# Loops over blocks in the first graph layer's sums, written out on four engines

## The chip, the cores and the metric

The kernel runs on one core of one Trainium2 chip. Time is device microseconds from the start to the end of one execution, and the lower the better. Five engines work side by side, each with its own list of instructions: PE (matrix products), DVE (vector), ACT (scalar and activation), POOL (here it issues the gathering DMAs) and SP (here it issues all other DMAs). They meet at semaphores.

## The reference, cut to what matters

Four graph layers run one after the other on 6250 nodes of 128 features and 200,000 edges. The change is in the first, a gated update from weighted means over neighbours in both directions:

```python
neigh1 = _weighted_mean_agg(feat, w, src, dst, n)   # sum of w * feat[src] by dst, over sum of w
neigh2 = _weighted_mean_agg(feat, w, dst, src, n)   # sum of w * feat[dst] by src, over sum of w
hn = jnp.concatenate([neigh1 @ W1.T, neigh2 @ W2.T], axis=1)
gi = hn @ w_ih.T + b_ih
gh = feat @ w_hh.T + b_hh
...
return nn_ + z * (feat - nn_)
```

The code's own name for the stage is stage_gru_sums: it makes the two sums (msum and wsum) for every node, in both directions.

## The kernel before, in words

The edges lie sorted by their target. They are cut into cells of up to 128 edges, where each cell has two target nodes, and 64 cells make a batch: NBATCH is 74, and the stage goes through the 74 batches in order. For a batch of number n, there are 16 steps q (HALVES), and this is what happens in them.

- Cells. DVE builds one-hot matrices for 8 cells at a time (L733, L738, L743: koh, loh, kw). PE multiplies them (make_cells, L813 to L821), four cells in each step q, into ps_cell. ACT copies the result to X (L798), a ring of 8 slots. SP stores X to the chip's memory, turned (store, L621 to L625): 16 stores of 196 KB for a batch, and each counts up one of four semaphores `stored`, a quarter of the batch each.
- Backward. SP loads the stored batch again, in another order, as AT (load_turned, L627 to L632): 8 loads of 392 KB, numbers 0 to 5 in the steps q = 9 to 14 of the same batch, numbers 6 and 7 in the steps q = 1 and 2 of the next. Load 6 waits for the last quarter, which means for the landing of store 15. With all eight landed, PE multiplies AT by the gathered target rows (backward, L823 to L833): 17 groups for a batch, from step q = 6 of the next batch on. DVE adds each group to x (L700).
- Forward. POOL gathers the source rows (L672), ACT makes one-hots and weights rows (L774, L777, L783), PE sums them (sum_run, L835 to L844, six for each batch), DVE adds to fwd (L717) at a bucket's number that it loads from memory into a register (run_bucket, L551 to L555).

Each engine has a function body(i, bb), which issues the whole work of batch n = 2 i + bb on this engine; the function asks known(n) to leave out batches that there aren't. over_bodies (L606) calls it. For i = 0 and 1 the calls are made while the program is written, so that n is a whole number and every column and semaphore value is a constant. From i = 2 to 36 over_batches (L528) makes a loop of the engine (`eng.Fori`) round two calls (bb = 0 and 1). There i is a register: each semaphore value that depends on n is worked out by the engine's sequencer ahead of the wait (ALU_OP, FUSED_REGOPS), as are the columns in key_tab, lo_tab, w_tab and run_save. At its end the loop has one branch back. For i = 37, which only finishes what is left of batch 73, the calls are written out again. POOL's list has no loop: it is written out for all 74 batches.

The order in which the work of an engine stands is written by hand, and there is no planner. SP's queue is one list, in which a load that waits holds up the stores behind it.

Of the kernel before, what the change touches and what calls it, by code (L numbers as in the profile page):

```python
# [45 lines left out]
NBATCH = -(-(ET + GROUPS - 1) // HALF)  # L46
# [72 lines left out]
def build(nc, a, out_x):  # L119
# [10 lines left out]
    def sem(name):  # L130
        stage_sems.append(nc.alloc_semaphore(name))
        return stage_sems[-1]
# [26 lines left out]
    with es:  # L159
# [368 lines left out]
        def over_batches(eng, body, tail=None, peeled=1):  # L528

            for i in range(peeled):  # L530
                for bb in range(2):
                    body(i, bb)
            with eng.Fori(peeled, NBATCH // 2) as i:
                for bb in range(2):
                    body(i, bb)
            if tail is not None:
                tail()
# [19 lines left out]
        def stage_gru_sums(fwd, key_tab, lo_tab, w_tab, dst_tab):  # L557
# [5 lines left out]
            with ExitStack() as ctx:  # L563
# [26 lines left out]
                runs_in = [sem(f"g_runs_in{b}") for b in range(2)]  # L590
                rows_in = [sem(f"g_rows_in{b}") for b in range(GR)]

                def known(n):

                    return not isinstance(n, int) or 0 <= n < NBATCH
# [8 lines left out]
                    return range(TG * k, min(TG * (k + 1), BUCKETS))  # L604

                def over_bodies(eng, body):  # L606
                    over_batches(eng, body, peeled=2)
                    for bb in range(2):
                        body(NBATCH // 2, bb)

                with nc.Block() as block:
                    @block.sync
                    def _(sp):
                        def load_runs(n, bb):

                            if not (isinstance(n, int) and n < 2):
                                sp.wait_ge(weighted, RPB * (n - 1))
                                sp.nop(nofuse=True)
                            sp.dma_start(runs[:, bb, :, :], run_save[:, :, bass.ds(n * RD, RD)]).then_inc(runs_in[bb], 16)

                        def store(n, bb, q):  # L621

                            sp.wait_ge(evacd, HALVES * n + q + 3)
                            sp.dma_start(turn_save[bb, CQ * q:CQ * (q + 1), :, :].rearrange("c k l -> k c l"),
                                         X[0:KEYS, q % XR, :].rearrange("k (c l) -> k c l", c=CQ)).then_inc(stored[q // QT_HALVES], 16)  # L625

                        def load_turned(m, b, y):  # L627

                            sp.wait_ge(stored[y // 2], 16 * QT_HALVES * (m + 1))
                            sp.nop(nofuse=True)  # L630
                            sp.dma_start(AT[y:P:EIGHTHS, b, :],
                                         turn_save[b, HALF // EIGHTHS * y:HALF // EIGHTHS * (y + 1), :, :].rearrange("c (j h) l -> (c j) (h l)", j=GRP)  # L632
                                         ).then_inc(turned[b], 16)

                        def body(i, bb):
                            n = 2 * i + bb
                            if known(n):
                                if isinstance(n, int) and n == 0:
                                    load_runs(n, bb)
                                if known(n - 2):  # L640
                                    sp.wait_ge(turned[bb], 16 * EIGHTHS * i)
                                    sp.nop(nofuse=True)
                            for q in range(HALVES):
                                if known(n):
                                    store(n, bb, q)
                                if q in (1, 2) and known(n - 1):
                                    load_turned(n - 1, 1 - bb, EIGHTHS - 3 + q)
                                if known(n) and 9 <= q < 15:
                                    if q == 9 and known(n - 2):
                                        sp.wait_ge(rev_made, TGS * (n - 1))  # L650
                                        sp.nop(nofuse=True)
                                    load_turned(n, bb, q - 9)
                                if q == 5 and known(n) and known(n + 1):
                                    load_runs(n + 1, 1 - bb)

                        over_bodies(sp, body)
                        sp.wait_ge(runs_in[0], 16 * (NBATCH // 2 + 1))

                    @block.gpsimd
                    def _(g):  # L660
# [24 lines left out]
                    def _(v):  # L685
# [62 lines left out]
                        def body(i, bb):  # L748
                            n = 2 * i + bb
                            for cc in range(CB):  # L750
# [7 lines left out]
                                add_run(n_then, s + 1)  # L758

                        over_bodies(v, body)  # L760

                    @block.scalar
                    def _(s):
# [23 lines left out]
                        def body(i, bb):  # L787
                            n = 2 * i + bb
                            for q in range(HALVES):
# [9 lines left out]
                                if known(n):  # L799
                                    if q in OH_AT:  # L800
                                        make_run_oh(i, n, bb, OH_AT[q])
                                    if q in SCALE_AT:
                                        weigh_run(n, bb, SCALE_AT[q])

                        over_bodies(s, body)

                    @block.tensor
# [1822 lines left out]
```

## Time and profile before

| | us |
|---|---|
| median of 3 runs | 9322.11 |
| lowest and highest run | 9304.29, 9326.89 |
| profiled execution, its own time | 9326.77 |
| its span (first to last instruction) | 9325.0 |
| PE, DVE, ACT, POOL busy in it | 8295.5, 5838.0, 5420.3, 4943.9 |

The profile's page has a picture of 40 slices, 233 us each, with busy shares in tenths. The stage of the change takes slices 1 to 12: it starts at about 125 us with the first loads, and its last backward group starts at 2805 us. PE's digit is 9 from slice 2 on in it, and DVE's and DMA's 8. The row of a stretch shows the same in numbers: busy us of each engine with the number of its instructions, then the granted TensorE clock (PEclk, 1 is full speed), the mean share for which the 16 DMA engines were busy, and GB/s. PE shows matrix products, PEld the weight loads beside them; an engine's name with a q is its sequencer. In a list in order of time, the bracket says how long the engine had been idle before, and who ended it.

### The profile page before, as it was taken

The numbers are of one execution on the slowest core, as the hardware profiler recorded it, in microseconds if no ns is written. First come the engines' busy times: TensorE is split into PE (matmuls) and PEld (weight loads), VectorE is DVE, ScalarE is ACT, GpSimd is POOL, SyncE is SP. The second block draws the span as 40 slices with busy tenths as digits, with TensorE's granted clock in tenths as the row PEclk, the third lists the DMA queues.
The fourth block names the chain that finished last, engine by engine and source line by source line (L and its number), as shares of the span: only waits on it lengthen the run. The fifth ranks groups of instructions, "written<-read, shape, count | busy, mean of one in ns | idle before, by whom it ended". The sixth has DMA issues, their size and how long they took to land. (4 is left out here: it accounts for less than half of the span.)

```text
span 9325.0 us, 221484 instructions
## 1 busy us (share of the span) xinstructions
PE 8295.5 (89%) x54969; PEld 6586.8 (71%) x54970; DVE 5838.0 (63%) x12428; ACT 5420.3 (58%) x14197; POOL 4943.9 (53%) x5229
## 2 busy tenths in 40 slices
PE   5999999989897999989988888888885999999998
PEld 4888888888884777766656666666663666666666
DVE  6888888888885777751145555555554555555555
ACT  5777777777774444430026767676754555555555
POOL 5666666666660000000007777777760777777775
PEclk8999999999998999999989999999997999999999
DMA  6888888888881222235544444444430222222222
GB/s 193 224 227 226 227 224 227 226 226 227 225 226 43 111 110 117 110 125 192 190 143 116 118 118 118 118 118 118 118 112 28 74 73 73 73 73 73 73 73 69
DMA packets 963534, 1294.60 MB, mean 139 GB/s; under 512 B 187018, under 2 KB 821186, under 8 KB 934210
## 3 DMA queue, kind: packets, MB, share of 16 engines
q1 hardware_dynamic: 769858, 837.45, 30.7%
q0 software_dynamic: 193536, 455.41, 17.7%
q8 instruction: 73, 1.20, 0.1%
q14 instruction: 67, 0.55, 0.0%
HBM read 906.61 MB, written 385.62 MB: 139 GB/s over the span
## 5 line engine op out<-in xcount | busy, mean ns | idle before, releaser
L1823 POOL DMA_INDIRECT x<-table,p_gidx x1632 | 1546.5, 948 | 2377.7 <-ACT p_gidx L1860 1957.9
L672 POOL DMA_INDIRECT g_G<-table,g_runs x1776 | 1686.5, 950 | 769.9 <-issue 479.5
L2275 POOL DMA_INDIRECT c_G<-table,c_gidx x1632 | 1548.4, 949 | 505.2 <-issue 497.1
L820 PE MATMUL g_ps_cell<-g_loh,g_kw 128*98 128x128 f32 x9472 | 1254.1, 277 | 29.2 <-DVE g_kw L743 29.2
L831 PE MATMUL g_ps_rev<-g_hrow,g_AT 128*128 128x129 f32 x7252 | 1054.6, 284 | 192.3 <-DMA g_AT<-turn_save 155.1
L820 PEld LDWEIGHTS g_ps_cell<-g_loh,g_kw 128*98 128x98 f32 x9472 | 1127.5, 168 | 29.7 <-DVE g_kw L743 29.4
L1913 PE MATMUL p_ps_sum<-x 128*96 128x256 f32 x3264 | 898.4, 398 | 231.5 <-DVE hid L1849 221.3
L798 ACT COPY g_X<-g_ps_cell 98x512 f32<-98x512 f32 x1184 | 681.4, 576 | 720.8 <-PE g_ps_cell L820 697.9
L831 PEld LDWEIGHTS g_ps_rev<-g_hrow,g_AT 128*128 128x128 f32 x7252 | 930.2, 197 | 239.9 <-issue 184.0
L1913 PEld LDWEIGHTS p_ps_sum<-x 128*96 128x96 f32 x3264 | 468.7, 163 | 646.0 <-ACT x L1878 260.3
L1849 DVE TENSOR_TENSOR hid<-hid,p_ps_sum 96x256 f32 x1632 | 678.0, 415 | 375.2 <-DVE hid L1849 372.1
L1840 DVE TENSOR_TENSOR x<-x,p_ps_pre 128x512 f32<-128x512 f32 x816 | 524.1, 684 | 498.0 <-DMA x<-table,p_gidx 493.4
L1385 ACT CAST a_A<-a_ps_cell 128x392 bf16<-128x392 f32 x1184 | 511.0, 492 | 542.7 <-PE a_ps_cell L1419 542.7
L1903 PE MATMUL p_ps_pre<-own,p_lhs 128*128 x3264 | 785.6, 384 | 9.9 <-issue 1.7
L2339 ACT ACTIVATE c_pos<-c_ps_lin,c_b 128x512 f32<-128x512 f32 x408 | 280.5, 688 | 872.5 <-PE c_ps_lin L2362 872.5
L700 DVE TENSOR_TENSOR x<-x,g_ps_rev 128x387 f32<-128x387 f32 (+1 forms) x1258 | 639.8, 535 | 228.5 <-PE g_ps_rev L831 228.3
L2314 DVE TENSOR_TENSOR acc<-acc,c_ps_sum 96x128 f32 x1632 | 462.5, 283 | 410.2 <-DVE acc L2314 354.7
L738 DVE TENSOR_TENSOR g_loh<-lo_tab,g_ps_row 128x1024 f32<-128x1024 f32 (+1 forms) x592 | 718.2, 1213 | 0.0
L1406 PE MATMUL a_ps_slot<-parts,a_A 128*128 128x384 bf16 x3626 | 683.1, 328 | 0.0
L1903 PEld LDWEIGHTS p_ps_pre<-own,p_lhs 128*128 128x128 f32 x3264 | 588.6, 190 | 101.9 <-issue 37.2
L1498 PE MATMUL a_ps_slot<-parts,a_A 128*128 128x384 bf16 x3626 | 603.2, 327 | 10.5 <-DMA a_A<-adj_save 10.5
L2380 PE MATMUL c_ps_sum<-c_G,c_oh 128*96 128x128 f32 x3264 | 455.0, 282 | 164.5 <-DVE c_G L2305 164.0
(344 smaller groups left out, 15168.1 us busy)
## 6 DMA issues: line engine op xcount, KB each, us to landing
turn_save<-g_X SPq DMA_DIRECT2D x1184, 196.0 KB
g_AT<-turn_save SPq DMA_DIRECT2D x592, 392.0 KB
adj_save<-a_A SPq DMA_DIRECT2D x74, 1568.0 KB, 5.1
a_A<-adj_save SPq DMA_DIRECT2D x74, 1568.0 KB, 6.6
c_ed<-in_edge_dram SPq DMA_DIRECT2D x1632, 25.0 KB
g_G<-table,g_runs POOLq DMA_INDIRECT x1776
p_lhs<-in_edge_dram SPq DMA_DIRECT2D x1632, 16.0 KB
x<-table,p_gidx POOLq DMA_INDIRECT x1632
```

What stands on the lines that cost most here:

```text
L672: g.indirect_dma_start(G[:, e % GR, q, 0:D], None, table, bass.IndirectOffsetOnAxis(ap=runs[:, n % 2, 0, RQ * e + q:RQ * e + q + 1], axis= ...
L700: v.tensor_tensor(rev[:, at.start:at.stop, :], rev[:, at.start:at.stop, :], ps_rev[(back + n_parity[0] + k) % 2][:, 0:len(at) * (D + 1)].r ...
L738: v.tensor_tensor(loh[:, b % NOH0, :, :], lo_tab[:, cells].unsqueeze(2).to_broadcast([P, CP, P]), row.unsqueeze(1).to_broadcast([P, CP, P] ...
L798: s.copy(X[0:KEYS, q % XR, :], ps_cell[q % 2][0:KEYS, :]).then_inc(evacd, 1)
L820: last = pe.matmul(ps_cell[q % 2][0:KEYS, r * P:(r + 1) * P], kw[:, b, cell, :], loh[:, b, cell, :], start=True, stop=True)
L831: last = pe.matmul(ps_rev[(b + k) % 2][:, t * (D + 1):(t + 1) * (D + 1)], AT[:, b, hi * P:(hi + 1) * P], hrow[:, b, :], start=True, stop=True)
L1406: last = pe.matmul(ps_slot[bb][:, 0:3 * D], A[:, bb, GRP * hi:GRP * (hi + 1), :].rearrange("p j c -> p (j c)"), parts[:, hi, :, :].rearran ...
L1823: g.indirect_dma_start(G[:, H * b + q, :], None, table2, bass.IndirectOffsetOnAxis(ap=gidx[:, b, q:q + 1], axis=0)).then_inc(gathered[b], 16)
L1849: v.tensor_tensor(hid[0:BN, at, :], hid[0:BN, at, :], ps_sum[q // 2][0:BN, q % 2 * 2 * D:(q % 2 + 1) * 2 * D].rearrange("p (o d) -> p o d" ...
L1903: last = pe.matmul(ps_pre[b % 2 * 2 + q // 2][:, q % 2 * 2 * D:(q % 2 + 1) * 2 * D], lhs[:, b, q, :], own[:, bass.ds(bucket[q], 1), :].rea ...
L1913: last = pe.matmul(ps_sum[k][0:BN, q % 2 * 2 * D:(q % 2 + 1) * 2 * D], oh[:, b, q, :], G[:, H * b + q, :], start=True, stop=True)
L2275: g.indirect_dma_start(G[:, H * b + q, :], None, table, bass.IndirectOffsetOnAxis(ap=gidx[:, b, q:q + 1], axis=0)).then_inc(gathered[b], 16)
```

## The change

The function over_bodies no longer calls over_batches. It calls body(i, bb) for all i from 0 to 37 while the program is written. So on SP, DVE, ACT and PE there is no loop in this stage, no register for i, and no branch; n is a whole number for all batches. The load of the run's numbers for a batch 74, which the loop issued although there is no such batch, is left out by known(n + 1), and the last wait of SP counts one load less. POOL's list is as it was. The bucket number of run_bucket is still loaded to a register, from an address that is now a constant. No other stage is changed.

```diff
                 def over_bodies(eng, body):
-                    over_batches(eng, body, peeled=2)
-                    for bb in range(2):
-                        body(NBATCH // 2, bb)
+                    for i in range(NBATCH // 2 + 1):
+                        for bb in range(2):
+                            body(i, bb)
...
                         over_bodies(sp, body)
-                        sp.wait_ge(runs_in[0], 16 * (NBATCH // 2 + 1))
+                        sp.wait_ge(runs_in[0], 16 * (NBATCH // 2))
```

## Rows read from the trace of the kernel before

**Rows 1.** Busy time by stretch of the stage; the columns stand in the first row.
```profile
core 0: us, PE busy (x) PEld busy (x) DVE busy (x) ACT busy (x) POOL busy (x), PEclk, DMA share, GB/s
...
1000.00:2000.00 1000.00, 907.12 (x7690) 878.62 (x7689) 834.40 (x1346) 736.59 (x1963) 665.76 (x702) 0.98 0.87 227
```

**Rows 2.** Waits, 370 to 2790 us: in total, times, longest.
```profile
PE g_ps_rev L831 <- DMA g_AT<-turn_save: 149.5, 67, 3.9
...
DVE fwd L717 <- issue: 96.8, 254, 0.8
...
PE g_ps_rev L831 <- DVE x L700: 22.4, 137, 0.9
```

**Rows 3.** PE in order of time, in the loop: start, length, what, idle before.
```profile
374.39 0.93 PE L831 MATMUL g_ps_rev<-g_hrow,g_AT 128*128 128x129 f32 x6 [1.07 <-DMA g_AT<-turn_save]
...
409.92 0.93 PE L831 MATMUL g_ps_rev<-g_hrow,g_AT 128*128 128x129 f32 x6 [2.78 <-DMA g_AT<-turn_save]
...
2773.55 0.93 PE L831 MATMUL g_ps_rev<-g_hrow,g_AT 128*128 128x129 f32 x6 [1.27 <-DMA g_AT<-turn_save]
```

**Rows 4.** SP's queue in order of time, around the end of a batch in the loop.
```profile
1539.94 4.96 SPq L624 DMA_DIRECT2D turn_save<-g_X  x3
1548.81 0.48 SPq L631 DMA_DIRECT2D g_AT<-turn_save  x1
1549.40 0.50 SPq L624 DMA_DIRECT2D turn_save<-g_X  x1
1549.99 0.48 SPq L631 DMA_DIRECT2D g_AT<-turn_save  x1
```

**Rows 5.** PE in order of time, same stretch.
```profile
1556.31 0.93 PE L831 MATMUL g_ps_rev<-g_hrow,g_AT 128*128 128x129 f32 x6 [2.31 <-DMA g_AT<-turn_save]
```

**Rows 6.** Line L533, the loop's own instructions, on SP and PE: min/median/max ns.
```profile
L533 SPq COMPARE_BRANCH  x35: 40/45/54, 359.7 to 2793.1; - x35
...
L533 PEldq COMPARE_BRANCH  x35: 76/208/233, 358.9 to 2791.9; - x35
```

**Rows 7.** Lines L826 and L623, 359 to 2793 us: register work ahead of waits.
```profile
L826 PEldq ALU_OP  x1054: 32/32/32, 360.4 to 2789.4; - x176
...
L623 SPq ALU_OP  x1020: 32/33/37, 361.9 to 2792.4; - x170
```

**Rows 8.** DMA queues, 284 to 359 us: packets, MB, share of 16 engines.
```profile
q8 instruction: 4, 0.07, 0.4%
q14 instruction: 5, 0.04, 0.2%
```

**Rows 9.** DMA queues, 359 to 2793 us.
```profile
q14 instruction: 14, 0.11, 0.0%
q8 instruction: 1, 0.02, 0.0%
```

**Rows 10.** DMA queues, whole span.
```profile
q8 instruction: 73, 1.20, 0.1%
q14 instruction: 67, 0.55, 0.0%
```

**Rows 11.** PE in order of time, batches written out already.
```profile
191.50 0.91 PE L831 MATMUL g_ps_rev<-g_hrow,g_AT 128*128 128x129 f32 x6 [1.59 <-issue]
...
227.10 1.63 PE L831 MATMUL g_ps_rev<-g_hrow,g_AT 128*128 128x129 f32 x6 [2.96 <-issue]
...
263.34 0.91 PE L831 MATMUL g_ps_rev<-g_hrow,g_AT 128*128 128x129 f32 x6 [2.07 <-issue]
...
303.01 1.65 PE L831 MATMUL g_ps_rev<-g_hrow,g_AT 128*128 128x129 f32 x6 [3.61 <-DMA g_AT<-turn_save]
```

**Rows 12.** Busy time by stretch, single batches; columns as in group 1.
```profile
191.50:227.10 35.60, 31.61 (x274) 30.61 (x275) 29.58 (x48) 26.55 (x71) 23.44 (x26) 1.00 0.87 231
...
263.30:303.00 39.70, 33.52 (x274) 32.34 (x274) 29.70 (x48) 26.15 (x70) 26.96 (x28) 0.94 0.84 206
374.40:409.90 35.50, 31.80 (x274) 30.65 (x274) 29.59 (x48) 26.98 (x73) 25.01 (x27) 1.00 0.91 234
```

## The prediction

> **What bounds the kernel now.** I read the stretches first, to see how steady the stage is; then the waits, which name what PE stands still for; then PE and SP in order of time, which show the round that sets the pace; and last the queues of the DMA with the loop's own line, because the change trades register work against instructions that must be fetched.
>
> In the stage PE is busy for 91% of the time and the DMA engines for 87% [rows 1]. The stage repeats itself: PE's first backward group of a batch starts at 374.39 us for the first batch that I count and at 2773.55 us 67 batches later [rows 3], so one batch takes 2399.16 / 67 = 35.81 us. That group nearly always has to wait for the loaded batch (AT), 149.5 us for 67 times, or 2.2 us a batch. PE waits 22.4 us for DVE's additions, 0.3 us a batch. DVE's 96.8 us of "issue" ahead of its addition to fwd are the load of the bucket number; DVE has slack (834 of 1000 us busy [rows 1]), and the load stays in the changed kernel [rows 2].
>
> The 2.2 us are the end of a round that goes through all of the pace. SP issues store 15 at 1539.94 us, load 6 can go only at 1548.81, when this store has landed, load 7 at 1549.99, and PE begins at 1556.31 [rows 4, 5]. From store 15 to PE's start these are 16.4 us, of which 8.9 are the landing of the store, 1.2 the way from load 6 to load 7, and 6.3 the landing of load 7. The rest of the round, 35.8 - 16.4 = 19.4 us, is PE's own work from the group to the last cells of the next batch. So anything saved in either part shortens a batch, and so does anything added lengthen it. What a batch does on SP's queue beside this path, on DVE, ACT and POOL, is covered.
>
> **What goes.** (a) The loop's own instructions. 35 branches on each engine, a median of 0.045 us on SP and 0.208 us on PE [rows 6]. On SP the branch stands behind store 15, where SP then waits for the next cells; on PE the sequencer is ahead of the products. Cost on the path nothing; were the cover gone, 35 x 0.21 = 7 us. I take 0.
>
> (b) Register work ahead of waits. On SP it is 33 ns for a store, 1020 of them, and on PE 32 ns, 1054 of them for one wait alone [rows 7]. Most of it is done while the sequencer waits anyway, or while the array has work in its queue. On SP's part of the path there is one place: load 6 ends at 1549.29 and store 1 begins at 1549.40 [rows 4], a gap of 0.11 us with one such instruction in it. At most the 0.11 go, at least nothing; I take the two thirds that are nearest to the instruction with its own hand-over, 0.06 us x 70 batches = -4 us.
>
> For PE's part there is a direct look, because batches 0 to 3 are written out already. The batch from 191.50 to 227.10 takes 35.60 us with 2.96 of stall, so 32.64 of work [rows 11]; one in the loop takes 409.92 - 374.39 = 35.53 with 2.78 of stall, so 32.75 [rows 3]. Both ran at full clock [rows 12], so the difference of 0.11 us is the register work that shows, and where it shows is the waits on DVE. Bounds: nothing, and all of PE's waits on DVE (0.33 us a batch, 23 us). I take 0.11 x 70 = -8 us.
>
> (c) One load of 36 KB for a batch that isn't there, and a smaller last wait. PE's last backward groups wait for load 7, not for it; 0 us, at most -1.
>
> **What comes.** (d) The written-out lists have to be fetched. In the loop next to nothing is: 1 and 14 packets in 2434 us [rows 9], the 14 about what POOL's written-out list takes. So the loop's bodies stay where the engines read them. While the last written-out instructions and the first turn of the loop were fetched, from 284 to 359 us (2.1 batches), there were 4 packets of 16 KB and 5 of 8 KB, with 0.4% and 0.2% of 16 engines [rows 8]: 4.8 and 2.4 us of one engine's time, 1.2 and 0.5 us a packet. For each batch this makes 1.9 and 2.4 packets, of which 0.2 of the small ones are POOL's and are there in any case; 1.9 x 1.2 + 2.2 x 0.5 = 3.4 us of one engine's time. Spread evenly over 16 engines, it is 0.21 us, and as the engines are busy for 87%, 0.18 us of this meets other transfers. x 70 = +13 us. Lower bound 0: packets that fall between loads cost nothing. Upper bound: all packets on one engine, and this one the last in every landing; 16.4 of 35.8 us are landings, so 3.4 x 0.46 = 1.6 us a batch, +109 us. I take +13, nearer to the low end, because the batch written out already that I looked at took no longer than the loop's (35.60 against 35.81 us).
>
> The Trainium skill ("Runtime: NRT & Kernel Launch", section "Instruction fetch mechanics") says that the instruction memory is a queue refilled in blocks of 16 KiB, 256 instructions, that crossing a block is "mostly hidden", and that a taken branch whose target is outside the two current pages stalls for the fetch of the target, for which reason it prefers full unrolling. On hidden crossings the trace agrees as far as it goes (the written-out batch of 32.64 us of work has no room for a stall that the loop lacks); on the branch it doesn't: PE's body holds two batches of 274 products and as many weight loads [rows 12], 1096, over four such blocks, and was not fetched again. By the rule, the change would gain what rival 3 below gives.
>
> **The sum.** -4 - 8 + 0 + 13 = +1 us against the execution's own 9326.77 us (span 9325.0 us), which is 4.7 us above the median of the runs. The stage's written-out batches as a direct measure say the same: 191.50 to 263.34 is 2 batches of 35.92 us, 0.11 above the loop's, +8 us. I forecast 9326 us, no difference that can be measured. A measurement of this kernel can tell about 0.3%, 28 us, from no change, which is 0.4 us a batch.
>
> **Rivals.**
> 1. Fetching lengthens the landings (slower). The mechanism is a fetched packet in front of the last piece of a store or of load 7; it decides from 0.6 us a batch on, where it has eaten (a) to (c) and 0.4 us. For it: batch 3, from 263.34 to 303.01, took 39.67 us with a stall of 3.61 [rows 11], with the DMA at 206 GB/s [rows 12]. With it the five batches from 191.50 to 374.39, all with fetching, take 36.58 us each, 0.77 above the loop's. x 70 = +54 us, 9381 us. Against it: in that stretch the clock was 0.94 against 0.98 [rows 1, 12], which lengthens PE's own part, and the two batches behind it, fetched too, take (374.39 - 303.01) / 2 = 35.69 us [rows 3, 11], less than the loop's.
> 2. The register work weighs more than I see (faster): all of PE's waits on DVE go (-23 us), SP's gap goes in full (-8), and an earlier load 7 keeps PE from the slow clock that follows long stalls. The batch from 227.10 shows what that is worth: its first group takes 1.63 us in place of 0.91, and the work of this batch is 36.24 - 2.07 = 34.2 us against 32.6, 1.6 us more [rows 11]. At one batch in ten more without it, -11 us. Together -42, 9285 us. Against it: the written-out batches still stall for 2.96 and 2.07 us.
> 3. Each branch back costs PE a fetch: then 35 x 6.3 us, the time in which a load lands, less the stall that hides 2.2 of each: -144 us, 9183 us. The branch's 0.208 us and the 1 packet speak against it.
> 4. PE outruns its fetches, as a packet has to get through DMA engines that are 87% busy. Each of 130 could cost up to the 6.3 us of a landing; at one in ten, +82 us, 9409 us. Against it: no such wait where fetching went on.
>
> That the change doesn't do what it says is the forecast itself, seen from its other side: the loop is taken away and nobody had been waiting for it.
>
> **How the numbers follow.** Forecast 0.60, rival 1 0.20, rival 2 0.13, rival 3 0.02, rival 4 0.05. The forecast's own range is 9298 to 9354 us. The range is 9280 to 9400: it takes in rivals 1 and 2, and leaves out 3, 4 and the far end of (d), somewhat over 0.1. Faster by over 0.3%: rivals 2 and 3 and a little of the forecast's edge, 0.16. Slower: 1 and 4, 0.24, as part of the forecast's edge and of rival 1's near end cancel. Within: 0.60.
>
> **What would show it.** In the changed trace the 16 KB queue has about 73 + 1.9 x 70 = 206 packets in place of 73, and the 8 KB queue 67 + 2.2 x 70 = 221 or fewer in place of 67 [rows 10]; the branches and nearly all ALU_OP of the stage are gone; the waits on DVE in PE's list fall from 0.3 us a batch to near 0; a batch takes 35.8 us within 0.4; the stall for AT stays near 2.2 us. Landings of store 15 well over 8.9 us with a stall of 3 us would be rival 1; waits of PE named "issue" in the middle of a batch would be rival 4; a batch of under 35.3 us would be rival 2 and prove my reading of the covers wrong.

## The result, and the profile after

| | before | after |
|---|---|---|
| median of 4 runs, us | 9321.03 | 9375.53 |
| lowest and highest, us | 9304.29, 9326.89 | 9364.66, 9383.33 |
| span of the profiled execution, us | 9325.0 | 9362.7 |

The ratio of after to before is 1.0061, with a 95% interval of 1.0043 to 1.0078: the changed kernel is slower by about 54 us. The forecast of the prediction (no difference, 9326 us) was not what came; its rival 1 (9381 us, chance 0.20) was.

The loops are gone and the lists are fetched. These are the DMA queues of the changed kernel over the whole span, which answer to [rows 10]:

```profile
q8 instruction: 222, 3.64, 0.2%
q14 instruction: 169, 1.38, 0.0%
```

73 packets of 16 KB became 222, and 67 of the small ones 169. The busy time in the stretch of [rows 1]:

```profile
core 0: us, PE busy (x) PEld busy (x) DVE busy (x) ACT busy (x) POOL busy (x), PEclk, DMA share, GB/s
...
1000.00:2000.00 1000.00, 887.95 (x7387) 859.83 (x7386) 801.62 (x1295) 706.94 (x1888) 636.91 (x674) 0.96 0.86 220
```

In the same 1000 us PE gets through 7387 products in place of 7690. (This stretch is a little worse than the stage, in which a batch takes 2.2% longer.) The DMA engines are about as busy (0.86 against 0.87), but move 220 GB/s in place of 227, and the granted clock is 0.96 in place of 0.98. PE's list in order of time shows the batches (against [rows 3] and [rows 11]):

```profile
225.48 0.91 PE L831 MATMUL g_ps_rev<-g_hrow,g_AT 128*128 128x129 f32 x6 [2.84 <-issue]
...
259.54 0.91 PE L831 MATMUL g_ps_rev<-g_hrow,g_AT 128*128 128x129 f32 x6 [1.43 <-DVE x L700]
...
368.85 0.91 PE L831 MATMUL g_ps_rev<-g_hrow,g_AT 128*128 128x129 f32 x6 [2.82 <-issue]
...
2784.03 1.63 PE L831 MATMUL g_ps_rev<-g_hrow,g_AT 128*128 128x129 f32 x6 [3.30 <-issue]
```

From 368.85 to 2784.03 are 66 batches of 36.59 us; before, it was 35.81. So 0.78 us x 70 batches = 55 us, which is the difference of the medians. Between the two profiled executions the difference is smaller, 9362.7 - 9325.0 = 38 us: the first group of the last batch starts 50 us later (2855.1 against 2805.3), and what follows, which is not changed, took 12 us less in this execution. (Where a wait's value is a constant, the trace often calls the wait for the loaded batch "issue"; it stands at the same place, the first backward group of a batch.) PE's waits from 370 to 2790 us, against [rows 2]:

```profile
PE g_ps_rev L831 <- issue: 168.3, 59, 4.7
...
PE g_ps_run L842 <- ACT g_Gw L783: 66.7, 139, 1.7
...
PE g_ps_rev L831 <- DVE x L700: 11.1, 7, 1.8
```

The 137 short waits on DVE are gone (the 7 that are left under this name are first groups of a batch), and the wait for the loaded batch is longer. It is the loads that end this wait, and not PE's own instructions: in the changed kernel PE begins 0.09 us behind the last landing of its batch's loads in each of the 67 batches, in the kernel before 0.14 us on average. One batch's end on SP and on PE, against [rows 4] and [rows 5]; here it is a mild one:

```profile
1561.16 5.01 SPq L624 DMA_DIRECT2D turn_save<-g_X  x3
1569.73 0.48 SPq L631 DMA_DIRECT2D g_AT<-turn_save  x1
1570.25 0.57 SPq L624 DMA_DIRECT2D turn_save<-g_X  x1
1570.91 0.48 SPq L631 DMA_DIRECT2D g_AT<-turn_save  x1
```
```profile
1577.03 0.91 PE L831 MATMUL g_ps_rev<-g_hrow,g_AT 128*128 128x129 f32 x6 [1.86 <-issue]
```

A single batch says little, as the landing of store 15 varies between batches (standard deviation 0.8 us before). So for each kernel I took the means over batches 5 to 71 of its one profiled execution, from these same lists: from the start of store 15 to that of load 6, from load 6 to load 7, from load 7 to PE's first backward group, PE's stall there, and the batch. The half clock is time at 1.2 GHz in place of 2.4, per batch, from the clock's records. All are in us:

| kernel | store 15 to load 6 | load 6 to 7 | load 7 to PE | stall | half clock | batch |
|---|---|---|---|---|---|---|
| before | 8.80 | 1.19 | 6.29 | 2.22 | 1.63 | 35.78 |
| after | 9.27 | 1.33 | 6.19 | 2.72 | 2.35 | 36.60 |

The standard error of each landing of store 15 is 0.1 us, so the 0.47 between them is clear of chance. The three parts of SP's path grew by 0.47 + 0.14 - 0.10 = 0.51 us. What this did to PE's batch can be added up from PE's own rows. The half clock counts with half of its time, as if the products in it took twice as long; "rest" is what is left, PE at work. (Counted so, the rest comes out alike where PE's and DVE's work is the same: 31.60 us before, 31.59 in pe_only_again and 31.57 in inj_small, both below.)

| PE, us a batch | stall for AT | half of the half clock | waits on DVE (L831) | waits for ACT's rows (L842) | rest | batch |
|---|---|---|---|---|---|---|
| before | 2.22 | 0.82 | 0.32 | 0.82 | 31.60 | 35.78 |
| after | 2.72 | 1.17 | 0.00 | 1.01 | 31.70 | 36.60 |

So the 0.82 us are +0.50 of stall, +0.36 of slow clock, -0.32 on DVE, +0.19 for ACT's rows and +0.09 of the rest. The waits on DVE that were saved came back, for the greater part, in the last two. The slow clock goes with the stall: in the trace before, 31 of the 67 stalls have a drop to half clock about their end (from 2 us before PE's first group to 1.5 us behind its start), and these are 2.71 us long on average, the others 1.81; in the changed trace it is 44 stalls of 2.99 us against 23 of 2.20.

### The profile page after: what moved, and what is told of

The parts are those of the page before. It is cut to its first block and busy times, and to the rows that moved or that the text cites. A ratio compares the mean times of both kernels' runs of the same rounds, so it can differ in the third digit from the quotient of the medians.

```text
span 9362.7 us, 211153 instructions
## 1 busy us (share of the span) xinstructions
PE 8309.1 (89%) x54969; PEld 6601.7 (71%) x54970; DVE 5831.8 (62%) x12428; ACT 5417.3 (58%) x14197; POOL 4932.3 (53%) x5229
## 5 line engine op out<-in xcount | busy, mean ns | idle before, releaser
L831 PE MATMUL g_ps_rev<-g_hrow,g_AT 128*128 128x129 f32 x7252 | 1062.9, 285 | 211.4 <-issue 191.2
L831 PEld LDWEIGHTS g_ps_rev<-g_hrow,g_AT 128*128 128x128 f32 x7252 | 938.7, 198 | 258.1 <-issue 201.3
L738 DVE TENSOR_TENSOR g_loh<-lo_tab,g_ps_row 128x1024 f32<-128x1024 bf16 x592 | 718.6, 1214 | 0.0
```

What stands on the lines that cost most here:

```text
L738: v.tensor_tensor(loh[:, b % NOH0, :, :], lo_tab[:, cells].unsqueeze(2).to_broadcast([P, CP, P]), row.unsqueeze(1).to_broadcast([P, CP, P] ...
L831: last = pe.matmul(ps_rev[(b + k) % 2][:, t * (D + 1):(t + 1) * (D + 1)], AT[:, b, hi * P:(hi + 1) * P], hrow[:, b, :], start=True, stop=True)
```

## The experiments

Theories: F, the lists, above all PE's, are now fetched by DMA, and this traffic lengthens the landings that PE waits for. Q, SP's constants change when its transfers are issued, and these collide otherwise. P, PE itself stands still for its instructions. The figures beside the runs are medians and the ratio to runs of the kernel before on the same chip.

**One engine's list at a time, first try.** over_bodies got an argument; SP's last wait is counted to match.

```diff
+                def over_bodies(eng, body, out=False):
+                    if out:
+                        for i in range(NBATCH // 2 + 1):
+                            for bb in range(2):
+                                body(i, bb)
+                        return
...
-                        over_bodies(pe, body)
+                        over_bodies(pe, body, True)
```

> The loop of this stage is written out on PE alone; SP, DVE and ACT keep it. Theory F (fetched packets of 16 KB, which belong to PE's list, stand in front of the landing of store 15 and of load 7): about 222 packets in the 16 KB queue, about 67 in the 8 KB queue, landing of store 15 near 9.2 us against 8.8, and nearly all of the loss: 9355 to 9370 us against 9321. Theory Q (SP, with constants, issues its stores and loads at other moments, and these collide differently): no loss, 9315 to 9325 us, since SP is in its loop. Theory P (PE itself stalls for its instructions): the same time as F, but with the landings unchanged and PE's idle time called issue in the middle of a batch.

> The loop is written out on SP, DVE and ACT, and PE keeps it. Theory F: 73 packets in the 16 KB queue, about 169 in the 8 KB queue; a small loss, 0 to +15 us against 9321, as the small packets take less than half the time of the large ones. Theory Q: the whole loss, 9365 to 9380 us. Theory P: no loss.

Two kernels with LATE = 6 were on the same chip:

```diff
-LATE = 5
+LATE = 6
```

> LATE is 6 in place of 5 in the kernel before: PE's first backward group of a batch comes one step q later, at q = 7, behind 1.5 us more of products. All loops stay. If the stall for the loaded batch (2.2 us a batch) closes the round that sets the pace, the stall falls to under 1 us and the kernel gains 1.5 us a batch and more where the clock no longer dips: 9321 - 74 x 1.5 = 9210 us, down to 9150. If another wait stands right behind (SP's load 0 at q = 9 waits for the end of the backward groups, which now ends one step later), it gains little, over 9290.

> LATE is 6 in the changed kernel, with all loops written out. Theory F: where PE has slack for the landings, their lengthening costs less: against late6_loop the loss is under 20 us in place of 54. If the loss were PE's own (theory P), or on another path than the landings, it would stay at about 54 us.

These four ran on another chip, on which the kernel before took 12337.74 us. pe_only took 12243.81 (ratio 0.993, 0.991 to 0.995), rest_only 12254.99 (0.9942, 0.9919 to 0.9964), late6_loop 12442.10 (1.0094, 1.0074 to 1.0113), late6_out 12250.74 (0.9936, 0.9916 to 0.9955). No expectation fits, since the kernel has another limit there. PE of late6_loop in order of time:

```profile
2009.79 0.94 PE L831 MATMUL g_ps_rev<-g_hrow,g_AT 128*128 128x129 f32 x6
2012.94 1.12 PE L820 MATMUL g_ps_cell<-g_loh,g_kw 128*98 128x128 f32 x8 [2.21 <-issue]
2015.80 1.66 PE L831 MATMUL g_ps_rev<-g_hrow,g_AT 128*128 128x129 f32 x6 [1.75 <-issue]
```

PE stands still for 2 us ahead of cells whose operands are there, again and again, at a mean clock of 0.86 over the run; the DMA engines are busy for only 61% in the stage, and PE's stall for the loaded batch is 0 in this trace. So these four runs say nothing on the landings. That writing lists out was worth 0.6 to 0.7% on such a chip, and 1.5% with LATE = 6 (12442.10 against 12250.74), is measured; why, stays open.

**The same kernels on a chip as before.**

> The same kernel as pe_only. That run met a chip on which the kernel before took 12338 us, with a granted clock of 0.87 and PE standing still inside rows of products, so that PE's pace hid the landings and the order of the times was another one. On a chip on which the kernel before takes about 9320 us, theory F (fetched 16 KB packets in front of the landings) expects 9355 to 9370 us, with 222 packets in the 16 KB queue; theory Q (the loss comes with SP's constants) 9315 to 9325 us.

> The same kernel as rest_only, for a chip on which the kernel before takes about 9320 us. Theory F: 73 packets of 16 KB and about 169 of 8 KB, 0 to +15 us, as 8 KB take less than half of the time of 16 KB. Theory Q: the whole loss, 9365 to 9380 us.

pe_only_again: 9354.01 us, ratio 1.0057 (1.0045 to 1.0069). rest_only_again: 9312.30 us, ratio 1.001 (1.0002 to 1.0019). The instruction queues, 359 to 2793 us, first with PE written out, then with the others:

```profile
q8 instruction: 148, 2.42, 0.4%
q14 instruction: 14, 0.11, 0.0%
```
```profile
q14 instruction: 120, 0.98, 0.1%
q8 instruction: 1, 0.02, 0.0%
```

So the 16 KB packets are PE's, and nearly all of the loss comes with PE's list: Q falls, as SP's constants alone cost 0.1%. P falls too: PE's waits in pe_only_again (370 to 2790 us) have none ahead of a cell, the long one is that for the loaded batch, and there PE begins 0.09 us behind the last landing in each of the 67 batches.

```profile
PE g_ps_rev L836 <- issue: 150.2, 58, 3.8
...
PE g_ps_run L847 <- ACT g_Gw L788: 55.2, 137, 0.8
...
PE g_ps_rev L836 <- DVE x L705: 34.8, 142, 1.7
```

In rest_only_again, the waits on DVE are the ones that are gone:

```profile
PE g_ps_rev L836 <- DMA g_AT<-turn_save: 151.4, 66, 4.3
...
PE g_ps_rev L836 <- DVE x L705: 2.0, 3, 0.9
```

| kernel | store 15 to load 6 | load 6 to 7 | load 7 to PE | stall | half clock | batch |
|---|---|---|---|---|---|---|
| pe_only_again | 9.06 | 1.33 | 6.04 | 2.44 | 2.09 | 36.23 |
| rest_only_again | 8.82 | 1.19 | 6.25 | 2.23 | 1.48 | 35.63 |

The landing of store 15 and the way from load 6 to 7 are longer with PE's list written out, and as before without. On the way from load 6 to 7 it is the issue of the one store between them that takes over 0.7 us, up to 1.6, in 14 batches of the changed kernel and 13 of pe_only_again; in the kernel before and in rest_only_again it never does. But the landing's 0.26 us are about two standard errors here, and load 7 to PE is 0.25 shorter, so the three parts together grew by 0.15 only. PE's account is clean: +0.22 of stall and +0.23 of slow clock are the whole 0.45, and its waits on DVE (0.32), those for ACT's rows (0.83) and the rest (31.59) are as before. (The profiled execution of pe_only_again is among its quicker ones, 9343 against a median of 9354.)

**Extra transfers in the kernel before.** If a 16 KB packet does the harm, it should do it where loops are kept. ACT issues a copy from the table to a scratch tensor, twice a batch:

```diff
+                                    if q in (15, 2):
+                                        s.dma_start(probe[bass.ds(2 * n + (15, 2).index(q), 1), 0:4096],
+                                                    table[0:32, :].rearrange("(o r) w -> o (r w)", o=1)[:, 0:4096]).then_inc(probed, 16)
```

inj_early has (7, 9) in place of (15, 2), inj_small 0:16 in place of 0:4096.

> The kernel before, all loops kept, and two extra DMAs of 16 KB for each batch, one row from the table to a scratch tensor that nobody reads, issued by ACT behind its copy of step q = 15 and behind step q = 2. So each falls into a landing that PE waits for: of store 15, or of load 7. Theory F says that a 16 KB packet in that place is what costs the time: +0.4 to +0.9 us a batch, 30 to 65 us over the kernel before. Theory P (PE's own fetching stalls it, transfers don't matter): 0 to 5 us.

> The same two DMAs of 16 KB for each batch, but behind the steps q = 7 and q = 9, where PE has just begun on the loaded batch and no landing is waited for. Theory F: they cost clearly less than in inj_land, 0 to 25 us. If the bytes alone counted, or the issue on ACT, they would cost the same as in inj_land.

> The same as inj_land with 64 B in place of 16 KB: the control for the issue on ACT and for the semaphore. All theories: within 15 us of the kernel before.

inj_land: 9310.65 us, ratio 1.0007 (0.9997 to 1.0016). inj_early: 9311.50 us, 1.0006 (0.9996 to 1.0015). inj_small: 9380.42 us, 1.0078 (1.0064 to 1.0092). The first two cost nothing that can be told, and the control was the dear one. The queue that ACT's copies use (359 to 2793 us; a packet of 4 B that tells of the landing goes with each piece), in inj_land and in inj_small:

```profile
q10 hardware_dynamic: 4324, 2.22, 0.4%
```
```profile
q10 hardware_dynamic: 4228, 0.02, 0.1%
```

Each copy is split into 16 pieces: 1 KB each, 46 ns by the median, in inj_land, and 4 B each in inj_small. A copy spread over 16 engines is no likeness of a fetched block, which is one packet of 1.1 us on average. So inj_land doesn't test F; it shows that two copies of 16 KB in this form don't count. In inj_small load 7 takes 6.93 us to PE in place of 6.29, and its stall is 2.75, 0.52 more than before; the half clock is 2.65, which costs 0.51 more, and the batch takes 36.77, 0.99 more. So a longer landing of load 7 is paid at the same place and in the same two parts as in the changed kernel:

```profile
PE g_ps_rev L837 <- DMA g_AT<-turn_save: 181.3, 66, 4.1
```

**One piece on one engine.** POOL gathers two rows of 12 KB, behind e = 2 of each batch.

```diff
+                                if e == 2:
+                                    g.wait_ge(probed, 16 * n)
+                                    g.indirect_dma_start(probe[:, :], None, table[0:48, :].rearrange("(a r) w -> a (r w)", r=24),
+                                                         bass.IndirectOffsetOnAxis(ap=probe_at[:, :], axis=0)
+                                                         ).then_inc(probed, 16)
```

> The kernel before, all loops kept, and one extra gather for each batch, issued by POOL behind the gathers of e = 2, about when store 15 is on its way: two rows of 12 KB from the table to a tile that nobody reads. inj_land's 16 KB came as 16 packets of 1 KB on 16 engines and cost nothing that could be told; here a row should stay one piece (or several) on one engine, as a fetched block does. Theory F: such a piece lengthens the landing of store 15 by 0.4 to 0.9 us and a batch by as much, 30 to 65 us. If single large packets don't matter: 0 to 10 us, the cost of POOL's issue, which has 4 us of slack a batch.

one_engine_land: 9298.80 us, ratio 0.999 (0.9981 to 0.9999). Each row did come as one packet of 12,288 B, of 0.46 us by the median, and it cost nothing in the time: store 15 to load 6 took 8.66 us. But the rows came late in this landing. They began 7.0 to 10.4 us behind the start of store 15, only 48 of 134 ahead of load 6, and nearly all ahead of load 7; and load 7 to PE took 6.50 us in place of 6.29 (standard errors 0.06). So what is refuted is that packets of this size, begun within some 1.7 us of load 6, cost 0.4 us and more. A packet in the first 7 us of store 15, or behind load 7, wasn't tried. Fetching also takes more of the engines: 2.2 packets x 1.1 us and 1.6 x 0.4 us (120 - 14 of the small ones over 2434 us), 3.1 us a batch against 2 x 0.5 here.

**The stall taken away.**

> The same kernel as late6_loop, for a chip on which the kernel before takes about 9320 us: PE's first backward group one step q later, loops kept. If the stall for the loaded batch closes the round that sets the pace, it falls from 2.2 to under 1 us, and the kernel gains 1.5 us a batch and more: 9210 us, down to 9150. If SP's load 0 at q = 9, which waits for the end of the backward groups two batches back, is the next limit, it stays above 9290.

> LATE is 6 and all loops are written out, on a chip on which the kernel before takes about 9305 us. In late6_loop_again the stall for the loaded batch was 0.14 us in place of 2.2 and the time 9288 us. Theory F: with this stall gone the landings have slack, and writing out costs under 20 us, under 9308 us. If writing out costs PE something else, the loss stays at 54 us, 9342 us.

late6_loop_again: 9287.77 us, ratio 0.997 (0.9958 to 0.9982). late6_out_again: 9285.65 us, ratio 0.9976 (0.9967 to 0.9985).

| kernel | store 15 to load 6 | load 6 to 7 | stall | half clock | batch |
|---|---|---|---|---|---|
| late6_loop_again | 7.90 | 1.19 | 0.14 | 0.97 | 35.48 |
| late6_out_again | 8.61 | 1.26 | 0.67 | 1.12 | 35.52 |

Writing out lengthens the landing here too, by 0.71 us (standard errors 0.09 and 0.16), but the batch by only 0.04. PE has a step of products more between, yet the stall still grows by 0.53 us, as much as in the given pair. What differs is that PE gets 0.45 us back in its waits on DVE (0.66 to 0.21) and 0.10 in those for ACT's rows, and that the slow clock costs only 0.08 more. So with another round setting the pace, as the next view suggests, a longer wait for AT takes the place of other waits. This fits theory F, and speaks against a cost that PE pays in any case; the place of the 54 us is shown better by PE's account in pe_only_again.

LATE = 6 itself gained 18 us by the medians and 28 by the ratio, where I had expected 110 and more. PE's and its suppliers' waits in late6_loop_again, 370 to 2790 us:

```profile
POOL g_hrow L678 <- PE g_ps_rev L831: 271.5, 67, 4.9
PE g_ps_run L842 <- ACT g_Gw L783: 143.6, 129, 2.7
ACT g_Gw L783 <- DMA g_G<-table,g_runs: 132.4, 61, 2.9
...
PE g_ps_rev L831 <- DMA g_AT<-turn_save: 7.6, 7, 1.8
```

The wait for AT is gone (149.5 to 7.6 us). But POOL's gather of the target rows waits for the end of the backward groups, and that now comes a step later. The gathers queued behind it are late, ACT waits for them (132.4 us, against none in this view before), and PE for ACT (143.6 against 55.2). The stall has turned into another. By their ratios these two kernels are 0.2 to 0.3% faster than the kernel before.

## Why the prediction was right and wrong

The time, 9375.53 us, lies in the range of 9280 to 9400, since the range took in rival 1; the case that I held likeliest is not the one that came.

- What bounds the kernel: right. The round from store 15 to PE's first backward group sets the pace, and where late6_out_again has another round, the same fetching costs the batch 0.04 us.
- (a), the branches: 0 was right as far as runs tell; rest_only_again has none of the branches on three engines and gains nothing. PE's own branch stands alone in no run; PE's waits and work in pe_only_again are as before.
- (b), register work: PE's part was misread. The waits on DVE do go, but with the lists of the other engines: 0.32 us a batch before and in pe_only_again, none in rest_only_again, so it wasn't PE's register work. Most of it came back, as +0.12 for ACT's rows and +0.12 in the rest in rest_only_again. By single batches the forecast seems to hold (225.48 to 259.54 has 34.06 - 1.43 = 32.63 us of work, 0.11 less than the 32.75 of the loop), but over 67 batches, less the stall and the slow clock, PE's part fell from 32.74 to 32.71 us, 0.03. SP's -4 us didn't come: load 6 to load 7 is 1.19 us in rest_only_again as before. In the rows above, the store begins 0.04 us behind the load's end in place of 0.11, but its issue takes 0.57 in place of 0.50, and it is so in rest_only_again too.
- (c): nothing to be seen of it.
- (d), fetching, is the step that failed, in its size. The counts were near: 222 packets against 206 forecast, 169 against at most 221. The price was not: I spread the engine time evenly over 16 engines, 0.18 us a batch or +13 us, where the landing of store 15 alone grew by 0.47 and the stall by 0.50. Load 6 waits for the last piece of store 15, and a mean over the engines says nothing of the last piece; so much is argument, as the runs show the growth and not the engine that it comes from. To it came the slow clock, which I had priced only as a gain for rival 2: PE runs at half clock beside the longer stalls (its first group takes 1.63 us, as at 2784.03), 0.36 us a batch. In all some 0.86 us, +60 us in place of 13.
- Why I chose the low end: one written-out batch of 35.60 us, and a mean over two. Rival 1's own estimate, from all five fetched batches ahead of 374.39 us, was 0.77 us a batch. The changed kernel has 0.78. I had put the excess down to the clock, as though that were apart from it, but slow clock and longer stalls go together. Still, that rival 1 met the size so well is luck. The same five batches, of which the first are the same program in all these kernels, took 36.58 us each in the trace before, but 35.77 in the changed one (190.01 to 368.85), 36.14 in pe_only_again and 36.24 in rest_only_again. The mean of the four, 36.18, is 0.37 above the loop's, and would have given +26 us.
- The Trainium skill ("Runtime: NRT & Kernel Launch", "Instruction fetch mechanics") calls the crossing of a block mostly hidden. For PE itself this agrees: no cell waits in pe_only_again, and its first groups begin 0.09 us behind the landing. What its list costs appears in the stores and loads that the fetches run beside.

What is shown: PE's written-out list causes nearly all of the loss (1.0057 against 1.001), and PE pays it at the wait for AT, which ends with a landing each time, and in the slow clock beside it (the whole 0.45 us of pe_only_again). That DMA traffic of the fetches is the link isn't shown by a run that adds such traffic alone: the added copies and gathers don't stand for it. Nor was it tried apart from the other thing that changes, that PE's list without registers issues at other moments; PE's own waits and work are as before there.

The link rests on the landing of store 15, longer in each of the three kernels that fetch PE's list, and on where the 16 KB packets fall. With one from 1 us before to 6 us after store 15 begins, its landing took 9.23 us in the changed kernel (42 batches), without 9.34 (25); but in pe_only_again 9.16 (40) against 8.90, and in late6_out_again 9.03 (36) against 8.13 (standard errors of the differences 0.26, 0.17, 0.30). With one in the same stretch about load 7, load 7 to PE took 6.81 us (11 batches) against 6.07 in the changed kernel and 6.53 (9) against 5.96 in pe_only_again (0.15 each), 7.13 (24) against 6.83 in late6_out_again (0.26). This speaks for the link, but weakly: the few batches were picked out afterwards, and in a stretch that begins 2 us before load 7 the difference is gone (6.15 against 6.22 in the changed kernel). How a packet acts stays open. What would fit is a queue that always uses the same DMA engine, whose backlog then ends last; no trace here names a packet's engine, and it wasn't tried.

## What to carry to other kernels

Before a loop is written out, look in the queues of the trace whether its body is fetched again at all: if it isn't, and the branch and register work stand beside waits, writing out takes away what nobody waits for and adds traffic. Ask then which landing closes the round that sets the pace, since there a few hundred nanoseconds count in full, and here the slow clock beside the longer stalls added 0.36 us to their 0.50. When several batches of the changed form are in the trace already, take the mean of all of them, and don't explain away the slow ones; but give the mean its spread, since that of five batches went from 35.77 to 36.58 us between four traces. And to learn which engine's list a wait hangs on, write them out one at a time: the waits of PE that I gave to PE's list were gone with the lists of the others.

## What was not expected of the hardware

- Two copies of 64 B a batch from memory to memory cost 75 us (1.0078), where two of 16 KB cost nothing that can be told (1.0007). Both are split in 16 pieces, here of 4 B to neighbouring addresses. The loads' packets of 25,088 B (359 to 2793 us) took 1607 ns on average in inj_small against 1504 before, and 3305 against 2314 at the 99th percentile. The Trainium skill ("DMA: Bandwidth & Descriptors", "Specifications") says that below 512 B the engines read, modify and write; that this happened here no run shows.
- A loop body of PE with 1096 products and weight loads went round 34 times with one packet fetched in 2434 us [rows 9, 12].
- On one of the chips the kernel before took 12338 us, with PE standing still for about 2 us at a time ahead of products that had all they needed, and there writing out lists gained 0.6 to 0.7%.
